# Two of the four diagonal-block copies move from SyncE's queue to ScalarE's, and the order of work around them changes on four engines

## What is computed

```python
mixed = silu(causal_conv4(xn @ W_qkv));  q, k, v = split(mixed)      # q, k l2-normalised
# per head, token by token
S = S * exp(g);  S = S + beta * k (v - k S)^T;  o = q S
o = o * rsqrt(mean(o * o) + 1e-6) * norm_w * silu(xn @ W_z)
out = o @ W_out
```

## Time and profile before

| | |
|---|---|
| median of three runs | 2795.55 us |
| profiled execution, device time | 2802.01 us |
| its span in the trace | 2800.1 us |
| TensorE matmul busy | 2619.4 us, 94% of the span |
| VectorE busy | 2001.6 us, 71% |
| ScalarE busy | 1610.8 us, 58% |
| GpSimd busy | 1075.5 us, 38% |

### The profile page before, as it was taken

How to read it: one execution, slowest core, us unless ns; L and a number is a source line. 1 busy time by engine, 2 the same in 40 slices (tenths; PEclk the granted TensorE clock), 3 DMA queues, 4 the chain that set the end, 5 groups by cost and what they waited for, 6 DMA issues and landing times.

```text
span 2800.1 us, 87430 instructions
## 1 busy us (share of the span) xinstructions
PE 2619.4 (94%) x34330; PEld 1946.0 (69%) x34330; DVE 2001.6 (71%) x4880; ACT 1610.8 (58%) x5046; POOL 1075.5 (38%) x1391
## 2 busy tenths in 40 slices
PE   2999997999999999999999999999999999999995
PEld 2456655777777777777777777777777777777774
DVE  5322235888878887888778877887778878888773
ACT  2111114666666666666666666666666666666662
POOL 0312203444444444444444444444444444444440
PEclk8999998999999999999999999999999999999997
DMA  4322301111111111111111111111111111111112
GB/s 148 76 53 64 64 1 53 46 54 46 53 46 54 46 54 46 54 46 54 46 53 46 54 46 53 47 43 49 43 49 50 49 49 50 50 50 50 50 50 64
DMA packets 225654, 146.99 MB, mean 52 GB/s; under 512 B 187456, under 2 KB 195936, under 8 KB 225120
## 3 DMA queue, kind: packets, MB, share of 16 engines
q1 hardware_dynamic: 219104, 123.58, 15.5%
q0 software_dynamic: 6144, 17.83, 2.8%
HBM read 115.81 MB, written 2.70 MB: 42 GB/s over the span
## 4 chain that ended last, share of the span: by engine, by line
PE 66%; DVE 8%; ACT 3%; issue 2%; DMA 2%; SPq 1%; POOL 1%; DVEq 0%; POOLq 0%; ACTq 0%
PE rps L809 12%; PE rps L734 8%; PE rps L742 8%; DVE conv L1262 6%; PE rps L696 4%; PE rps L826 4%; PE rps L713 4%; PE rps L865 3%; PE rps L856 3%; PE rps L839 3%; PE rps L680 3%; PE rps L706 3%; PE rps L774 3%; PE rps L783 3%; PE rps L683 2%
## 5 line engine op out<-in xcount | busy, mean ns | idle before, releaser
L1262 DVE SCALAR_TENSOR_TENSOR conv<-rps,w_in,conv 128x509 f32<-128x509 f32 (+2 forms) x768 | 572.0, 745 | 64.6 <-ACT conv L1050 46.4
L809 PE MATMUL rps<-xnT,w_in 128*128 128x512 f32 x1024 | 504.3, 615 | 13.9 <-DVE cols L1244 13.0
L1461 POOL TENSOR_TENSOR decay_b<-decay,beta_k 128x512 f32<-128x512 f32 x128 | 130.6, 1042 | 487.6 <-DVE beta_k L1278 487.6
L1412 POOL TENSOR_TENSOR o_t<-o_sq,q_mean 128x8 f32<-128x8 f32 x65 | 13.4, 206 | 691.0 <-ACT gated L983 691.0
L809 PEld LDWEIGHTS rps<-xnT,w_in 128*128 128x128 f32 x1024 | 174.8, 190 | 148.2 <-issue 125.2
L742 PE MATMUL rps<-w_z,xnT 128*128 128x256 f32 x1040 | 275.1, 387 | 1.0 <-ACT z L999 0.7
L1050 ACT ACTIVATE conv<-rps,w_in 128x512 f32<-128x512 f32 x256 | 176.1, 688 | 164.5 <-PE rps L809 161.5
L734 PE MATMUL rps<-w_outn,gatedT 128*128 128x256 f32 x1056 | 241.3, 381 | 1.0 <-ACT gatedT L993 0.7
L734 PEld LDWEIGHTS rps<-w_outn,gatedT 128*128 128x128 f32 x1056 | 201.6, 191 | 49.7 <-issue 23.8
L1064 ACT ACTIVATE qkT<-conv 128x512 f32<-128x512 f32 x128 | 80.5, 629 | 222.1 <-DVE conv L1262 222.1
L742 PEld LDWEIGHTS rps<-w_z,xnT 128*128 128x128 f32 x1040 | 183.1, 191 | 21.6 <-ACT z L999 1.1
(11 more groups left out here) (217 smaller groups left out, 6477.4 us busy)
## 6 DMA issues: line engine op xcount, KB each, us to landing
sums_row<-g_rows SPq DMA_DIRECT2D x65, 1024.0 KB, 5.0
scale<-comb_rows POOLq DMA_DIRECT2D x40, 256.0 KB, 5.0
w_in<-in_w_in SPq DMA_DIRECT2D x17, 520.0 KB, 3.5
bq<-bmat SPq DMA_DIRECT2D x256, 32.0 KB, 2.0
inv<-xq SPq DMA_DIRECT2D x256, 32.0 KB, 1.9
w_z<-in_w_z SPq DMA_DIRECT2D x17, 256.0 KB, 2.6
w_out<-in_w_out SPq DMA_DIRECT2D x17, 256.0 KB, 5.0
invT<-xqT SPq DMA_DIRECT2D x128, 32.0 KB, 2.2
```

What stands on the lines that cost most here:

```text
L809: last = nc.tensor.matmul(ps[PROJ_BANK[j]][:, :], w_in[:, m * 4 * P + j * P:m * 4 * P + (j + 1) * P], xnT[:, m, b * T:(b + 1) * T], start= ...
L1262: nc.vector.scalar_tensor_tensor(conv[:, j, shift:T], ps[PROJ_BANK[j]][:, 0:T - shift], w_in[:, k:k + 1], conv[:, j, shift:T], ALU.mult, A ...
L1461: nc.gpsimd.tensor_tensor(decay_b[:, us, :], decay[:, us, :], beta_k2[:, us].unsqueeze(2).to_broadcast([P, NC_, C]), ALU.mult).then_inc(db ...
```

## The change

Two of the four diagonal copies (blocks 2 and 3) are no longer issued by SyncE but by ScalarE, in a new piece `gather()` behind `take_updates(1)`. All four still count up the same semaphore. Besides, pieces change places on every compute engine. On TensorE, k_products(0) moves from before attend(1) to behind solve(2), read_state(2) moves ahead of project_z(0), and solve(2) ahead of project_z(1). On VectorE, compact moves behind residual(2). On GpSimd, k_norms moves ahead of mask_level(1). On ScalarE, take_transposes(0), silu(2), squares(0), take_updates(2) and take_v(0) move forward. No computing instruction is added or removed.

```diff
@@ SyncE
-                    for rows in BLOCKS:
+                    for rows in BLOCKS[:2]:
                         sp.dma_start(bq[rows, :, :], bmat[rows, :, rows]).then_inc(diag_in, 16)
@@ TensorE
                     by_token(2)
-                    k_products(0)
                     attend(1)
+                    read_state(2)
                     pe.wait_ge(wz_in, (i + (1 if b == 0 else 2)) * 16)
                     pe.wait_ge(tap_done, n(12) + 12)
                     project_z(tb, 0)
-                    read_state(2)
+                    solve(2)
+                    k_products(0)
                     project_z(tb, 1)
-                    solve(2)
                     spread_rows()
@@ ScalarE
+                    def gather():
+
+                        act.wait_ge(b_done, n(2) + 2)
+                        for rows in BLOCKS[2:]:
+                            nc.scalar.dma_start(bq[rows, :, :], bmat[rows, :, rows]).then_inc(diag_in, 16)
+
...
+                    take_transposes(n, 0)
                     take_updates(0)
                     first_tap(3)
-                    take_transposes(n, 0)
+                    silu(2)
                     take_transposes(n, 1)
-                    silu(2)
                     take_state_part(1)
                     take_updates(1)
+                    gather()
                     exp_decay((b + 1) % BATCH, n(4) + 8, n(2) + 2, 0)
                     squares_by_token(0)
+                    squares(0)
                     exp_decay((b + 1) % BATCH, n(4) + 8, n(2) + 2, 1)
+                    take_updates(2)
+                    take_v(0)
                     take_state_part(2)
-                    squares(0)
-                    take_updates(2)
                     silu(3)
-                    take_v(0)
                     take_merge(0)
@@ VectorE
                     output(1)
-                    compact()
                     decayed_k(0)
                     residual(2)
+                    compact()
                     decayed_k(1)
@@ GpSimd
                     rows8()
+                    k_norms()
                     mask_level(1)
-                    k_norms()
```

## The result

The changed kernel takes 2860.97 us (median of four runs, 2858.75 to 2866.72), against 2799.75 for the kernel before beside it. The ratio is 1.0217, with a 95% interval of 1.0204 to 1.023. That is 61 us slower; +60 was forecast, on a base of 2795.55.

What follows compares the result with a forecast made beforehand. TensorE's chain was taken to bound the kernel. 46 ordinary steps at 1.00 us (46 us) plus 18 late ones (14 us) gave +60 us, 2856 us from a median of 2795.6; 8-in-10 range 2822 to 2892 us.

Steps and rivals of the forecast that it cites:

- TensorE's order: TensorE idles before read_state(2), 1.00 us an ordinary step; spread_rows from S+7.75 to S+8.75, S being the first diagonal copy's start.
- The idle time that would be seen: Sign in the profile after: TensorE idle 0.7 to 0.9 us before line 680 every step, some 50 us together.
- ScalarE's issue: Two copies issued on ScalarE behind take_updates(1), at S+3.12 and S+3.76, taken as 0.64 us each, bounds nothing and 1.3.
- Late steps: 18 of 64 steps whose diagonal blocks come late and delay spread_rows: +0.8 us each, 14 us, between +0.32 and +1.31.
- Worth the late steps at most: VectorE's compact behind residual(2) uncouples the scan from the copies: gains at most 0.68 us a late step, 12 us.
- the dear part: TensorE's new order, k_products(0) and project_z(0) put after read_state(2): 1.00 us a step, 46 us over 46 ordinary steps.
- B: Rival: copies behind ScalarE land late and gate spread_rows, up to +186 us, milder form +95; chance 0.14 for 2885 and above.
- C: Rival: TensorE's gaps in the merges vanish in exchange, +4 to -8 us; chance 0.08, in part (+30) 0.06.
- D: Rival: compact's move pays and TensorE's order costs nothing, read_state(2) not waiting: -12 us, 2784; chance 0.01.

Runs made afterwards that it cites:

- e7: The changed kernel with all four diagonal copies back on SyncE and gather() not called: ratio 1.0174 to the kernel before, +49 us.
- e9: The kernel before with only the moves of order on ScalarE and GpSimd: ratio 1.0005 to the kernel before, +1 us.
- e4: The kernel before with only compact moved behind residual(2) on VectorE: ratio 1.0139 to the kernel before, +39 us.
- e1: The changed kernel with TensorE's order of before, all else as changed: ratio 1.0162 to the kernel before, +45 us.
- e2: The kernel before with only TensorE's new order: ratio 1.0219 to the kernel before, +61 us.

## Why the prediction was right

**TensorE's order is what the changed kernel pays for.** The working had read_state(2) at 1578.08 - 1573.36 = S+4.72 and spread_rows at S+8.75; the trace has 4.68 and 8.71. The forecast took 1.00 us for an ordinary step, and it is 0.96. e7 shows that the copies' place adds next to nothing to it, and e9 that the other moves add nothing.

**The idle time that would be seen was mis-sized.** I wrote 0.7 to 0.9 us before line 680 and some 50 us together; the trace prints 0.39 and 25.7 us. The loss is 0.96 by the starts. Line 713, ahead of it, starts at 1383.87 and is printed as busy for 0.61 us, but costs only 0.45 where work follows directly; the restart costs 0.1 more; and take_updates(1), which TensorE now waits for before line 706, costs the rest. A printed idle time behind a matmul is smaller than what was lost, as I had seen at line 696 (0.65 printed, 0.92 lost) and not carried over.

**ScalarE's issue** costs 0.64 us each, as taken. The first went out with the start of upd(1)'s read-out and not with its end, at S+2.69 in place of 3.12, so the blocks were there at S+5.41 in place of 5.82. It had cover anyway.

**Late steps.** I took 0.8 us for each of 18 of them, 14 us. The count was read wrongly: three of the 18 waits before line 696 stand in the kernel's end, so 15 steps of the loop had one. And the term was mis-sized: in the changed kernel 8 of 38 steps have late blocks, up to S+6.65, and the mean offset exceeds the ordinary one by 0.04 us. The 0.9 us in hand before line 847, 0.45 in my sum, swallow most of their lateness. Over all 64 steps the sum comes out as 64 x 0.96 = 61.4 us, less 11.0 us that the late steps cost before, and 4.2 us that they cost now: +54.6, where I had 46 and 14. The rest of the steps adds 3 us. The profiled executions differ by 57 us and the medians by 61, with an interval of 57 to 64. That 60 met 61 owes something to luck. The fixed 2.0 us of the Trainium skill (page DMA: Bandwidth & Descriptors, section Anatomy of one DMA), which I set beside this, is given there for transfers that GpSimd issues; SyncE's and ScalarE's copies here have a median of 2.0 us too, and single ones took up to 3.7 us before and 3.8 after.

**"Worth the late steps at most"** was right for compact in the changed kernel and only there. The prediction did not say that the move needs TensorE's new order, and that TensorE's order is partly what makes compact's new place bearable; e4 and e1 showed it. A reader who undid only "the dear part" would have won 16 us, not 60.

**Rivals.** B (the gather becomes the gate) did not occur: line 847 waits 1.8 us in all. C (gaps exchanged) did not occur in the changed kernel, where line 865's gaps are 26.8 us; in e2 some 14 us of it did. D (TensorE's order costs nothing) fell with the wait before line 680. Line 865 in the kernel before:

```profile
PE rps L865 <- issue: 26.0, 40, 1.2
```

By the Trainium skill, page DMA: Bandwidth & Descriptors, section Issuing engines are not separate DMA queues, issuing from several engines saves only the time of issuing. The trace agrees as far as it goes: the median from issue to landing stays 2.0 us, and about as many steps have late copies (8 of 38, against 11 of 40).

## What to carry to other kernels

Where several engines with fixed orders meet at one instruction, write down when each of them arrives there; a move is worth the change in the latest arrival, not the wait that it removes, and moves tried one by one don't add up. Before moving filler out from between a producer and its consumer, look when the producer can be ready at the earliest: of the 1.76 us of k_products(0) and project_z(0) in front of read_state(2), 0.96 had been free, because ScalarE and VectorE needed that time. A move off a busy queue gains nothing if the new issuer reaches the issue later than the old one would have ended all of its own.

## What the runs showed of the hardware

A transfer issued by ScalarE goes out while the instruction ahead of it has just begun: both stand at 1382.89. It then holds back the next instruction of ScalarE, here the table load, by 0.98 us of "issue" for two copies of 0.64 us. In the kernel before, without the copies, the table load started right behind the same instruction's end at 1576.44:

```profile
1576.45 1.28 ACT L1022 ACT_TABLE_LOAD   x1
```

In single cases an issue takes up to 1.4 us on ScalarE's queue in the kernel after, and up to 2.0 us on SyncE's in the kernel before.

The rest of a step, nearly the same work each time, takes 27.1 to 29.2 us. In the kernel before, steps in order give 27.6, 27.9, 29.0, 28.6, 27.1, 27.4, 27.1, 27.1, 27.1 and then 27.9, 29.0, 29.1, 29.2, 27.3, 27.2, 27.1, 27.1: a beat of eight or nine steps. The mean is 0.65 us above the least, 41 us over the loop, more than six of the ten experiments moved. Of this, 26 us are gaps of "issue" inside the small matmuls of the merges (line 865). The same beat is in every kernel, and in e2 it is weaker. What causes it was not tried.
